# Causal attention inside an adaLN block: the order of the key blocks in the second query half

## Time and profile before

| | |
|---|---|
| median of 3 runs | 2493.68 us (2493.58 to 2498.49) |
| profiled execution, its own time | 2495.66 us |
| its span | 2493.9 us |
| PE busy | 2406.7 us (97%) |
| DVE busy | 1723.4 us (69%) |
| POOL busy | 1650.8 us (66%) |
| ACT busy | 1042.6 us (42%) |

### The profile page before, as it was taken

How to read it: one execution, slowest core, us unless ns; L and a number is a source line. 1 busy time by engine, 2 the same in 40 slices (tenths; PEclk the granted TensorE clock), 3 DMA queues, 4 the chain that set the end, 5 groups by cost and what they waited for, 6 DMA issues and landing times. The chain is left out here.

```text
span 2493.9 us, 36376 instructions
## 1 busy us (share of the span) xinstructions
PE 2406.7 (97%) x13140; PEld 1668.3 (67%) x13204; DVE 1723.4 (69%) x3392; ACT 1042.6 (42%) x1873; POOL 1650.8 (66%) x865
## 2 busy tenths in 40 slices
PE   5999999999999999999999999998999999999998
PEld 3788888887555555555555555544788788888886
DVE  4866666677888888888888888874555355455553
ACT  3433333231666666666666666665211111111111
POOL 3744333441799998999989999993655455545643
PEclk8999999999999999999999999999999999999999
DMA  6532333352545325344233345313333333323330
GB/s 236 198 118 87 115 113 118 123 150 80 162 100 146 82 64 154 83 132 97 71 79 83 83 117 132 84 31 127 112 92 101 103 90 97 118 86 104 107 93 25
DMA packets 179727, 267.45 MB, mean 107 GB/s; under 512 B 20508, under 2 KB 113884, under 8 KB 178400
## 3 DMA queue, kind: packets, MB, share of 16 engines
q1 hardware_dynamic: 179552, 265.13, 36.2%
HBM read 183.22 MB, written 80.81 MB: 106 GB/s over the span
## 5 line engine op out<-in xcount | busy, mean ns | idle before, releaser
L1082 POOL TENSOR_TENSOR p_sum<-p_sum,p_ring 128x1024 f32<-128x1024 f32 (+2 forms) x465 | 991.3, 2164 | 71.0 <-PE ctx_ps L1143 50.2
L976 ACT ACTIVATE p_ring<-scores 128x512 f32<-128x512 f32 (+1 forms) x896 | 448.9, 568 | 236.3 <-DVE scores L1030 173.6
L272 DVE TENSOR_REDUCE neg_max<-scores_q 128x1 f32<-128x512 f32 x679 | 438.8, 684 | 79.0 <-PE scores_q L253 64.9
L253 PE MATMUL scores_q<-k_stack,q_stack 96*128 96x512 f32 (+1 forms) x1473 | 443.0, 378 | 14.6 <-DVE neg_max L269 6.3
L1122 PE MATMUL scores<-q_stack,k_stack 98*128 98x512 f32 (+1 forms) x1216 | 409.7, 414 | 10.6 <-ACT p_ring L976 7.7
L253 PEld LDWEIGHTS scores_q<-k_stack,q_stack 96*128 96x128 f32 x1473 | 263.6, 191 | 135.4 <-DVE neg_max L269 64.5
L1122 PEld LDWEIGHTS scores<-q_stack,k_stack 98*128 98x128 f32 x1216 | 205.9, 190 | 184.7 <-ACT p_ring L976 71.9
L627 POOL TENSOR_TENSOR roped_hilo<-roped_hilo 128x512 fp32r<-128x512 f32 x80 | 105.5, 1319 | 337.0 <-ACT roped_hilo L467 337.0
L269 DVE CUSTOM_DVE_ANT_0 scores_q<-scores_q,masks 128x512 f32<-128x512 f32 x489 | 296.0, 642 | 38.4 <-PE scores_q L253 38.4
L676 PE MATMUL proj_ps<-h_hi,w_hi 128*128 128x512 f32 x752 | 298.7, 397 | 0.7 <-POOL w_lo L616 0.7
L676 PE MATMUL proj_ps<-h_hi,w_lo 128*128 128x512 f32 x752 | 294.1, 391 | 0.0
(11 more groups left out here) (182 smaller groups left out, 3632.8 us busy)
## 6 DMA issues: line engine op xcount, KB each, us to landing
q_stack<-qk_t SPq DMA_DIRECT2D x96, 512.0 KB, 6.8
qk_t<-roped_hilo SPq DMA_DIRECT2D x80, 512.0 KB, 2.8
x_in<-in_L_attn_resid SPq DMA_DIRECT2D x32, 512.0 KB, 6.3
ctx_t<-ctx_raw SPq DMA_DIRECT2D x64, 256.0 KB, 5.4
prefetched<-in_L_wmod SPq DMA_DIRECT2D x4, 4096.0 KB, 13.6
prefetched<-ctx_t SPq DMA_DIRECT2D x31, 512.0 KB, 4.0
prefetched<-inv_t SPq DMA_DIRECT2D x124, 128.0 KB, 5.5
k_stack<-qk_t SPq DMA_DIRECT2D x96, 128.0 KB, 8.8
```

The lines of the kernel that those rows point to most:

```text
L253: last = nc.tensor.matmul(dst[:, a, :], qs[0:MHI, h, i * P:(i + 1) * P], ks[0:MHI, lo:lo + w], start=not first and (a == 0 or not diag), s ...
L272: nc.vector.tensor_reduce(neg, src, AX.X, ALU.max, negate=True).then_inc(sh.s_mx.sem, 1)
L976: nc.scalar.activation(p[:, a * per:(a + 1) * per, :], src[:, a * per:(a + 1) * per, :], ACT.Exp, scale=SM_SCALE).then_inc(s_ex.sem, 1)
L1082: nc.gpsimd.tensor_tensor(a, a, probs(n, u), ALU.add).then_inc(s_ap.sem, 1)
```

## The change

`KEY_ORDER` gives the order of the key blocks by half. The second half takes 0, 4, 1, 5, 2, 6, 3, 7 in place of 0 to 7. After it the units of the second half are: 6 and 7 block 0, 8 and 9 block 4, 10 and 11 block 1, 12 and 13 block 5, 14 and 15 block 2, 16 block 6, 17 and 18 block 3, 19 block 7. The diagonal ones among them are 8, 9, 12, 13, 16 and 19 in place of 14 to 19. The quads are numbered in this order, and the pairs of the values steps are now blocks 0 and 4 (at unit 11), 1 and 5 (unit 15), 2 and 6 (unit 18) and 3 and 7 (unit 1 of the next group). The end of an accumulation is now found by the last quad and no longer by the block's number.

```diff
+KEY_ORDER = [(0, 1, 2, 3), (0, 4, 1, 5, 2, 6, 3, 7)]
 EXP_UNITS = []
 for _hf in range(2):
-    for _j in range(4 * _hf + 4):
+    for _j in KEY_ORDER[_hf]:
...
-QUADS = [[u for u in range(NE) if EXP_UNITS[u][:2] == k] for k in sorted(set(e[:2] for e in EXP_UNITS))]
+QUADS = [[u for u in range(NE) if EXP_UNITS[u][:2] == k] for k in dict.fromkeys(e[:2] for e in EXP_UNITS)]
...
-                                                start=(j == 0), stop=(j == 4 * hf + 3))
+                                                start=(j == 0), stop=(q == LAST_QUAD[hf]))
```

## The result

The changed kernel takes 2545.64 us (median of 4 runs, 2541.32 to 2551.99) against 2493.63 (2492.98 to 2498.49): ratio 1.020, 95% interval 1.0178 to 1.0222. It is slower, as forecast, but by 52 us where 23 were forecast, and above the range. The profiled execution took 2543.22 us, 47.6 more than the one of before. The clearest mark of a group is the interval from one sending of the maxima to the next. In an ordinary group it takes 34.91 us against 33.50; 34.2 was forecast. Ordinary are 22 of the 31 intervals; the others hold the first or the last group, products for the modulation, or the reciprocal of the sums.

The account below looks back on a forecast made before the run. PE was taken to set the pace, in lock step with ACT and DVE. Shifts of PE around a group summed to 0.73 us, times 31 about 23 us, giving 2516 us; forecast case 2503 to 2528, wider range 2484 to 2532.

Parts of the forecast that it names:

- Units 8 and 9: Two masks come to DVE there, one falling into its idle time: +0.10 us a group, bounds 0 and 0.66.
- Units 12 and 13, the hold at unit 15: Unit 13's mask queues behind unit 12's reductions, so unit 15's scores wait: 0.65 us, bounds 0 and 0.9.
- Unit 16: Now block 6 with a 512-column mask; ACT's copy of the sums comes after its exponentials, +0.87 us.
- Units 17 to 0: Masks lost at 17 and 18; SP issues at +0.75 us, the maxima transfer holds unit 0, leaving +0.32.
- The fixed cost of a transfer: About 2.0 us from the skill, 2.6 with the second issue; the sum used the trace's 2.77 us.
- The step that failed: Unit 0 to unit 2: 3.13 us before, 3.55 forecast, with only the longer values step added.
- The values at unit 1: Blocks 3 and 7 replace 6 and 7, 1.20 us for 0.79: +0.41 us a group, bounds 0 and 0.43.
- A: Rival: DVE bounds units 14 to 5, spreading masks frees PE; up to 0.86 us a group faster, 2467 us; chance 0.17.
- C: Rival: each of four moved masks is a hold of its own, 1.30 us a group, 2534 us; chance 0.10.
- The high bound: All high bounds together, about +1.9 us a group; half of it over the forecast was taken, +1.3, 40 us.

Follow-up runs that it names:

- e3: Kernel before the change, with only the two masks of units 14 and 15 moved to units 8 and 9, values steps keeping their widths: 2502.94 us.
- e2: Kernel before the change, with only the two masks of units 14 and 15 moved to units 12 and 13, values steps keeping their widths: 2532.17 us.
- e6: Changed kernel with unit 13's mask ahead of unit 12's second reduction in DVE's order: 2530.22 us.
- e1: Changed kernel with the values of blocks 2 and 6 moved back from unit 18 to unit 19, between unit 19 and unit 0: 2520.35 us.
- e12: Changed kernel with unit 19's mask cut from 128 columns a head to 1, a timing probe with wrong output: 2535.12 us.
- e9: Kernel before the change, old order, with block 5's values moved from unit 19 to unit 1 of the next group: 2502.88 us.
- e5: Changed kernel with the reciprocal of the sums moved from unit 12 to unit 14: 2537.55 us.
- e7: Kernel before the change with key order 0 4 5 1 2 3 6 7, masks at units 8 to 11, 18 and 19, steps in place: 2503.84 us.
- e10: Kernel before the change, old order, with seven masks (units 1, 2, 3, 16 to 19) ahead of the previous unit's last reduction: 2629.24 us.

## Why the prediction was off

- **Units 8 and 9:** +0.11 against +0.10. Right; e3 shows it alone (+0.14).
- **Units 12 and 13, the hold at unit 15:** right in place, cause and size (+0.51 with the shorter values step, +0.45 forecast). e2 makes such a hold alone, e6 takes 0.44 us of it away by the order in DVE's queue.
- **Unit 16:** the copy of the sums came behind ACT's own exponentials, as forecast (they start at 1048.18, the copy at 1049.15; 0.87 us later in its group than before, as forecast).
- **Units 17 to 0:** the transfer took over at unit 0, 2.77 to 2.79 us after the issue in 23 of 30 groups, against 3.20 before. Right as an event; SP's issue was 0.15 us earlier than forecast (21.66 us after unit 6, 21.06 before, so +0.60 and not +0.75), and PE's shift at unit 0 was +0.18 and not +0.32. But the transfer doesn't set the pace there. In the seven other groups unit 0 came 2.90 to 4.18 us after the issue; in the six of them up to 3.21 us the values at unit 1 still came 5.97 to 5.98 us after it, when DVE's queue let them. So the +0.18 at unit 0 and the loss behind it are one hold by DVE's queue, split at unit 0.
- **The fixed cost of a transfer** in the Trainium skill, "DMA: Bandwidth & Descriptors", section on the anatomy of one DMA, gave an estimate of 2.6 us for the two issues; the trace has 2.77. The section's figure is for transfers that GpSimd issues, which the prediction doesn't say, and these are issued by SP; that it comes near is no test of it.
- **The step that failed** is the one from unit 0 to the values at unit 1. The prediction let it stand as it was before (3.13 us from unit 0 to unit 2, and only the 0.41 of the longer values step added) and put a hold by DVE there at nothing. Its reason was "After, DVE would be free in it", said of units 17 to 0, and "From unit 2 to 7 nothing changes" is the only word on what follows. DVE was indeed idle for 1.67 of the 4.83 us from unit 17 to unit 0, but ahead of unit 19 and not behind it. Before, DVE drained its queue during the values step between units 19 and 0, and the change had just moved that step away. Now unit 19's 512-column mask and two reductions come 0.8 us before unit 0's scores, and the values come 3.20 us after unit 0 in place of 2.34: the missing term is +0.86 us a group, 27 us in all. e1 (values step put back, 2.33 us) and e12 (mask cut, 2.83 us) show it, from PE's side and from DVE's.
- **The values at unit 1:** +0.42 against +0.41. Right. e9 shows that such a move counts in full at unit 1 and is paid back before unit 0 only down to the transfer.
- **Not foreseen:** the reciprocal ahead of unit 13's mask, with the fall of the clock, 5 us in the profiled execution and 8 us in e5. The changed kernel's runs also lie wider apart (11 us) than those of before (6 us), and they rank by the mean granted clock: 2541, 2543, 2548 and 2552 us at 0.989, 0.988, 0.985 and 0.984. That fits falls of the clock in more or fewer groups; it was not tested by itself.
- **The rivals:** A falls with e7: less DVE work at units 14 to 17 gave PE some 0.15 us. C was near in size, but for another reason; moved masks are not a hold each, as e3 and e7 show. The high bound was cut to half over the forecast without a row for the cut. Uncut, at +1.9 us a group, it would have held the result, but by luck: it had no term for this queue.

With the missed term the sum would have been 0.73 + 0.86 = 1.59 us a group, and less 0.15 for SP's issue 1.44, against 1.40 measured.

## What to carry to other kernels

When a long step of one engine is moved, ask what it was giving the others time for: here a values step on PE was the pause in which DVE emptied its queue before the next group. A diagonal block costs little where its mask falls into idle time and two long steps lie ahead of the scores that need its buffer, and a lot where it stands behind reductions and the next wait is two units away. Walk a lock step all the way round, with each engine's queue, until the state at the end is that of the start. And where two waits end near each other, here a transfer and a queue, only the one that ends last is worth shortening.

## What was not expected of the hardware

The granted clock fell to 0.50 after PE had been without work for 1.91 us in a stretch otherwise full, in e3, e6 and e9 after 1.37 us, and in e10 after 0.87 and 1.14 us with 1.2 us of work between them. The length of such a gap doesn't decide alone. In group 16 of the changed kernel PE waited 1.90 us in the same place and the clock stayed at 1.00, so the same hold cost 0.12 us there and 3.31 in group 24; and before the change, and in e7, it stayed at 1.00 after 1.37 us in all three of the reciprocal's groups. What decides between them is not shown by any run here.
